# A graph kernel's bf16 parts made inside its projection loop, its sums cleared by GpSimd, and a destination group's extra tiles made in a loop of single turns

## The reference

```python
def gcn_conv(x, W, b, src, dst, norm):          # src, dst with a self loop for each node
    h = x @ W
    return segment_sum(h[src] * norm[:, None], dst, num_segments=N) + b

deg = segment_sum(ones, dst);  dinv = rsqrt(deg);  norm = dinv[src] * dinv[dst]
h = maximum(layernorm(x), 0)
h = relu(gcn_conv(h, W1, b1)); h = relu(gcn_conv(h, W2, b2))
x = x + gcn_conv(h, W3, b3)
h = maximum(layernorm(x), 0)
hv   = h @ W_pre.T + b_pre
filt = edge_attr_50 @ W_rad.T + b_rad
h    = segment_sum(hv[src] * filt, dst, N)
out  = x + silu(h @ W_post.T + b_post)
```

## Time and profile before

| What | us |
| --- | --- |
| median of 3 runs (lowest, highest) | 6050.92 (6018.92, 6109.7) |
| profiled execution, its own time | 6113.65 |
| span of the profiled execution | 6111.8 |
| PE busy (matmuls) | 4563.4 |
| DVE busy | 3084.6 |
| POOL busy | 2929.8 |
| ACT busy | 946.0 |

### The profile page before, as it was taken

How to read it: one execution, slowest core, us unless ns; L and a number is a source line. 1 busy time by engine, 2 the same in 40 slices (tenths; PEclk the granted TensorE clock), 3 DMA queues, 4 the chain that set the end, 5 groups by cost and what they waited for, 6 DMA issues and landing times.

```text
span 6111.8 us, 111789 instructions
## 1 busy us (share of the span) xinstructions
PE 4563.4 (75%) x31388; PEld 3521.4 (58%) x31389; DVE 3084.6 (50%) x8559; ACT 946.0 (15%) x2182; POOL 2929.8 (48%) x3028
## 2 busy tenths in 40 slices
PE   6955777888888885999876999556666666566665
PEld 4742234555555565888665888355555555555554
DVE  6766777777777764444435444542222222222225
ACT  0000123344455541000020000010000000000002
POOL 0002133444510002666715666347777777777772
PEclk9966999999999995999858999566666666666665
DMA  1000011212211111455313554212222222222221
GB/s 33 0 11 18 27 43 50 64 59 70 71 60 68 73 55 49 157 168 169 104 47 104 170 171 150 38 45 48 46 46 46 48 46 46 46 46 48 46 46 33
DMA packets 158668, 407.12 MB, mean 67 GB/s; under 512 B 67564, under 2 KB 80940, under 8 KB 139124
## 3 DMA queue, kind: packets, MB, share of 16 engines
q1 hardware_dynamic: 62068, 305.32, 14.1%
q0 software_dynamic: 96256, 98.76, 8.6%
HBM read 307.53 MB, written 96.33 MB: 66 GB/s over the span
## 4 chain that ended last, share of the span: by engine, by line
PE 41%; POOL 25%; issue 17%; DVE 11%; DVEq 4%; DMA 1%; SPq 0%; POOLq 0%; ACT 0%; ACTq 0%
POOL rows_flat L510 25%; PE ps L1267 13%; PE ps L1366 6%; PE ps L1379 5%; PE ps L1340 5%; PE ps L1239 5%; DVE sumT L974 4%; PE ps L1256 3%; PE ps L1254 2%; PE ps L1247 2%; PE ps L1225 1%; DVE stage_fn L691 1%; DVEq L1048 1%; DVEq L691 1%; DVE hot L1205 1%
## 5 line engine op out<-in xcount | busy, mean ns | idle before, releaser
L510 POOL DMA_INDIRECT rows_flat<-table,row_stage x3008 | 2916.6, 970 | 2060.7 <-issue 1775.6
L1247 PE MATMUL ps<-hot,msg_flat 128*64 128x160 f32 x3136 | 810.8, 446 | 723.2 <-DVE msg_flat L795 723.2
L1366 PE MATMUL ps<-sumT,stage_fn 128*128 128x392 f16 x3976 | 866.3, 338 | 369.3 <-DVE sumT L974 228.0
L1247 PEld LDWEIGHTS ps<-hot,msg_flat 128*64 128x64 f32 x3136 | 650.4, 215 | 839.1 <-issue 707.1
L974 DVE TENSOR_SCALAR sumT<-stage_fn,sub_start,sumT 128x784 f16<-128x784 f16 x1988 | 895.7, 483 | 0.8 <-issue 0.7
L1366 PEld LDWEIGHTS ps<-sumT,stage_fn 128*128 128x128 f16 x3976 | 312.9, 98 | 901.5 <-issue 609.7
L1267 PE MATMUL ps<-wide,ring 128*128 128x192 bf16 x9800 | 828.3, 246 | 0.0
L587 ACT ACTIVATE ring<-ps 128x784 fp8e4<-128x784 f32 x800 | 657.1, 822 | 1047.9 <-PE ps L1366 1033.4
L1267 PEld LDWEIGHTS ps<-wide,ring 128*128 128x128 fp8e4 x9800 | 805.5, 98 | 8.5
L685 DVE TENSOR_SCALAR hot<-iota,dst_rel 128x160 f32<-128x160 f32 (+1 forms) x3008 | 656.2, 294 | 217.0 <-issue 214.5
L795 DVE TENSOR_TENSOR msg_flat<-rows_flat,ps 128x512 f32<-128x512 f32 x196 | 134.6, 687 | 1017.5 <-DMA rows_flat<-table,row_stage 995.9
(11 more groups left out here) (162 smaller groups left out, 2878.6 us busy)
## 6 DMA issues: line engine op xcount, KB each, us to landing
ring<-counts SPq DMA_DIRECT2D x100, 1568.0 KB
counts<-ring SPq DMA_DIRECT2D x50, 1568.0 KB
rows_flat<-table,row_stage POOLq DMA_INDIRECT x3008
ring<-in_radial SPq DMA_DIRECT2D x196, 200.0 KB
table<-node SPq DMA_DIRECT2D x56, 224.0 KB, 1.9
out<-node SPq DMA_DIRECT2D x13, 224.0 KB
ring<-in_dst SPq DMA_DIRECT2D x1, 784.0 KB
ring<-in_src SPq DMA_DIRECT2D x1, 784.0 KB
```

Source lines behind the costliest of these rows:

```text
L510: nc.gpsimd.indirect_dma_start(out=rows[:, j, k * D:(k + 1) * D], out_offset=None, in_=table[:, :], in_offset=bass.IndirectOffsetOnAxis(ap ...
L1247: s = nc.tensor.matmul(to, of, mats[:, k, :], start=(k == 0), stop=(k == BLOCK_TILES - 1))
L1366: m = nc.tensor.matmul(to[:, c, :], sources[:, :, k], joint[k][:, c * (JOINT // 2):(c + 1) * (JOINT // 2)], start=first, stop=True, skip_g ...
```

## The change

Three edits. First, `project(p)` of layers 0, 1 and 2 makes the parts of a group of windows right behind that group's L1011, inside the same loop; the loop of its own behind it is gone. Second, `sumT` is no longer cleared by DVE: POOL does it, after ACT has staged the last sums of the layer before (`fn_staged`) and ahead of its wait for the table, and DVE waits for the new semaphore `sums_cleared` before the pass. Third, the extras of a sub are made by one loop with one turn in each round, on DVE and on PE. All extras of a sub go to the extra buffer `a % 2`, where a is the sub's number modulo 4; before, pairs of turns alternated between the two buffers, and an odd last one went to buffer 0.

```diff
@@ -282,6 +282,7 @@
         root_wanted = sem("root_wanted")
         root_ready = sem("root_ready")
         sums_done = sem("sums_done")
+        sums_cleared = sem("sums_cleared")
         h_ready = sem("h_ready")
         nf_staged = sem("nf_staged")
         flipped = sem("flipped")
@@ -527,6 +528,9 @@
             pool.wait_ge(mode_ready, 1)
             for p in range(PASSES):
                 at = Pass(pool, p)
+                if p:
+                    pool.wait_ge(fn_staged, (COLLECT(p - 1) + 1) * GROUPS)
+                    nc.gpsimd.memset(sumT[:, :], 0.0).then_inc(sums_cleared, 1)
                 pool.wait_ge(table_written, 16 * GROUPS * (p + 1))
                 with pool.If(at.rounds > 0) if p == REDO else nullcontext():
                     with pool.Fori(0, at.rounds) as i:
@@ -1003,6 +1007,26 @@
                 return ps_z[:, h, 0:GROUP * D].rearrange("p (w f) -> p w f", f=D)
 
             def project(p):
+                settle()
+                at = steps[0]
+
+                def parts_of(g2, h, mine):
+
+                    part = [parts[:, groups(g2 * 2 + h), c * D:(c + 1) * D] for c in range(3)]
+
+                    def after(k):
+                        dve.wait_ge(step, g2 * 8 + (at + h * 4 + k))
+
+                    dve.wait_ge(z_used, g2 * 2 + (PROJECT(p) * GROUPS + h + 3))
+                    after(0)
+                    nc.vector.tensor_copy(part[0], mine).then_inc(step, 1)
+                    after(1)
+                    nc.vector.tensor_tensor(tmp[:, :, :], mine, part[0], ALU.subtract).then_inc(step, 1)
+                    after(2)
+                    nc.vector.tensor_copy(part[1], tmp[:, :, :]).then_inc(step, 1)
+                    after(3)
+                    nc.vector.tensor_tensor(part[2], tmp[:, :, :], part[1], ALU.subtract).then_inc(step, 1)
+
                 with dve.Fori(0, GROUPS // 2) as g2:
                     for h in range(2):
                         mine = node[:, groups(g2 * 2 + h), :]
@@ -1010,30 +1034,11 @@
                         if p < GCN_LAYERS:
                             nc.vector.tensor_tensor(mine, z, over_features(dinv[:, groups(g2 * 2 + h)]),
                                                     ALU.mult).then_inc(z_used, 1)
+                            parts_of(g2, h, mine)
                         else:
                             nc.vector.tensor_tensor(mine, z, over_windows(bias[:, B_PRE, :], GROUP),
                                                     ALU.add).then_inc(z_used, 1)
-                if p:
-                    then(nc.vector.memset(sumT[:, :], 0.0))
-                settle()
                 if p < GCN_LAYERS:
-                    at = steps[0]
-                    dve.wait_ge(z_used, (PROJECT(p) + 1) * GROUPS + 2)
-                    with dve.Fori(0, GROUPS) as g:
-                        mine = node[:, groups(g), :]
-                        part = [parts[:, groups(g), c * D:(c + 1) * D] for c in range(3)]
-
-                        def after(k):
-                            dve.wait_ge(step, g * 4 + (at + k))
-
-                        after(0)
-                        nc.vector.tensor_copy(part[0], mine).then_inc(step, 1)
-                        after(1)
-                        nc.vector.tensor_tensor(tmp[:, :, :], mine, part[0], ALU.subtract).then_inc(step, 1)
-                        after(2)
-                        nc.vector.tensor_copy(part[1], tmp[:, :, :]).then_inc(step, 1)
-                        after(3)
-                        nc.vector.tensor_tensor(part[2], tmp[:, :, :], part[1], ALU.subtract).then_inc(step, 1)
                     steps[0] += 4 * GROUPS
                     settle()
                     dve.drain().then_inc(parts_ready, 1)
@@ -1053,12 +1058,8 @@
                         made = joint_hot(joint_main[a][k], sub, t0 + k)
                     made.then_inc(main_ready, 1)
                     with dve.If(n > 0):
-                        with dve.If(n > 1):
-                            with dve.Fori(0, n >> 1) as m2:
-                                for b in range(2):
-                                    extra_hots(b, sub, extra_tile(t0, m2 * 2 + b))
-                        with dve.If((n & 1) > 0):
-                            extra_hots(0, sub, extra_tile(t0, n - 1))
+                        with dve.Fori(0, n) as m:
+                            extra_hots(a % 2, sub, extra_tile(t0, m))
 
             def keep_found(i, h):
 
@@ -1143,6 +1144,7 @@
             for p in range(PASSES):
                 if p:
                     project(p)
+                    dve.wait_ge(sums_cleared, p)
                 if p < GCN_LAYERS:
                     dve.wait_ge(table_written, 16 * GROUPS * (p + 1))
                 edge_pass(p)
@@ -1410,12 +1412,8 @@
 
                     with pe.If(n > 0):
                         main_begins()
-                        with pe.If(n > 1):
-                            with pe.Fori(0, n >> 1):
-                                for b in range(2):
-                                    extra_tiles(to, b)
-                        with pe.If((n & 1) > 0):
-                            extra_tiles(to, 0)
+                        with pe.Fori(0, n):
+                            extra_tiles(to, a % 2)
                         main_ends()
                     with pe.Else():
                         main_begins()
```

## The result

The kernel before takes 6080.47 us (median of 20 runs, 6015.8 to 6137.39), the changed one 6104.13 (median of 20, 6071.31 to 6125.48). The ratio is 1.007 with a 95% interval of 1.0043 to 1.0097: 42 us longer, 26 to 59. The ratio leaves out the runs that lie more than 1.5% above the fastest of their kernel, five of before's 20 and none of the changed kernel's; the medians of all runs lie 24 us apart, their means 27. The forecast was 6101, 50 us above the 6050.92 known then, and no change that 2% could tell.

A forecast was written before the change was run, and what follows sets the result against it. No engine owns the span, so stages were priced at three places. Terms -39.6 - 86.8 + 0 + 191 + 14 - 14 - 15 sum to +50 us on a median of 6050.92, giving 6101 us; range 6000 to 6180.

The forecast's parts named there:

- Part 1, layer 0, -39.6: Layer 0's projection: parts fit in DVE's idle time, so the build starts at 491.2 instead of 530.82, -39.6 us.
- the closing condition: End of the prediction: wrong if turns on one buffer come under 1.5 us apart, or another engine takes the projections' saved time.
- Layers 1 and 2, -43.4 each: Projection to dense pass: parts end sooner, gathers are late next, PE starts 43.4 us earlier per layer, -86.8 in all.
- Part 2, 0 in layer 3, no cost beside DVE: POOL clearing sumT: layer 3 gains 0 (-4 to 0) as gathers set its pace; the memset costs DVE 0.
- Turns, +191: Build loop: 196 later extra turns wait for PE on one buffer, 1.83 or 1.50 us each, +191 us.
- Lost lead, +14: Build loop: DVE cannot run ahead over subs with two or more extras, +14 us (0 to +30).
- First extras' waits, -14: Build loop: a sub's first extra uses another buffer than its neighbour's, so waits less for PE, -14 us (-27 to 0).
- Code, -15: Build loop: shorter code, 749 rows for 1197, removes the later stop but not the jump's stop, -15 us (-34 to 0).
- low clock: Rival, build loop: PE stays at 1.2 GHz through three rounds, all 196 turns cost 1.83 us; +144, 6195 us; chance 0.10.
- Turns covered: Rival, build loop: 2.4 GHz throughout, no lead lost, first waits and later stops gone; -38, 6013 us; chance 0.19.
- The jump's stop goes: Rival, build loop: 749 rows fit, so 25 stops of 4.8 to 8.7 us go; +50 - 69, 6032 us; chance 0.08.
- GpSimd's memset stops DVE: Rival, clearing of sumT: POOL's memset stops DVE or comes late; +32, 6133 us; chance 0.05.

The follow-up runs named there:

- e2: Kernel before with only the parts moved inside the projection's loop, DVE still clearing sumT behind it; 5992.56 us, ratio 0.9892.
- e8: Kernel before, unchanged, run once more for another profile; 6018.41 us in one run.
- e3: Changed kernel with the pair loop of before for the extra tiles, so only parts and clearing moved; 5960.4 us, ratio 0.9853.
- e6: Changed kernel plus a never-entered pair loop in each sub of DVE's code, restoring the loop's 1197 rows; 6154.04 us, ratio 1.0178.
- e4: As e3, but a sub's pair loop and odd tile begin on buffer a%2 instead of buffer 0; 5947.0 us, ratio 0.9823.
- e1: Kernel before with only the single-turn loops for extra tiles on DVE and PE; 6194.14 us, ratio 1.0237.
- e9: As e3, with the third part of each node value left out and its array cleared once; 5964.39 us, ratio 0.9819.

## Why the prediction was right

It was right in size, and luck had a share in it twice. The 6101 is +50 on a median of three runs, 6050.92, that lay 30 us below the median of 20; the same +50 on 6080.47 would be 6130. And the change itself, +50 for a measured +24 to +42, is a sum whose two large parts missed in opposite directions: Parts 1 and 2 gain less than forecast, Part 3 costs less.

- *Bound by stages, three places.* Held.
- *Part 1, layer 0, -39.6.* Measured -39.5 where both projections run at 1.2 GHz (e2), -20.6 where the one without parts would have run at 2.4 (e8's 79.2 us against 58.6 from first product to first main tile). The step that failed is "PE is not held up, and the cover is DVE's idle 4.11 us". It is true of layers 0 to 2 in the profile of before, which had drawn 1.2 GHz; at 2.4 GHz a group is 2.6 us on PE and 3.6 on DVE (the forecast had 3.8), DVE is the bound, and then the clock goes too. So the closing condition, that another engine picks up the time that the projections give back, was met in part, by PE.
- *Layers 1 and 2, -43.4 each.* The mechanism held to 2 us (45.6 at 1.2 GHz, gathers late next), its size again only at that clock; from 147.6 to some 120 it is 27.
- Weighing both cases by the 7 of 12 draws at 2.4 GHz, -39.6 and -86.8 become about -28 and -70: **-98 instead of -126**. e3 measured -89 (64 to 113), by the means -105.
- *Part 2, 0 in layer 3, no cost beside DVE.* Held.
- *Turns, +191.* The sum of turns rose by 204. The turn itself was priced 0.09 us too long at either clock (1.74 and 1.41, not 1.83 and 1.50). By its own words the prediction is wrong if turns on one buffer come closer than 1.5 us, and at 2.4 GHz they do: "a turn costs what a pair did" is not exact. The sum is above +191 all the same, because the clock was up only from the second half of the second round on, not from sub 16.
- *Lost lead, +14.* Measured 0: e6 against e4, 203.8 us in the loop for 203.1 in the turns (subs 0 to 127).
- *First extras' waits, -14.* e4 has -17 in its loop.
- *Code, -15.* The term that was mis-sized: e6 puts it at **50 us**. The stop at the jump stayed, as forecast, and the later one went. But that one had been misread: it is not in some ten rounds and five subs on, but in three, two subs on, 9.3 us in all. What the term left out is that the stops at the jump became shorter too, by 26.5 us over all 24.
- Together for Part 3, 204 - 17 - 50 - 13 (the last unexplained) is the **+124** of the loops, **instead of +176** (e1: +143 by its ratio, +125 by the means). With -98 that is +26; e1 and e3 together are +54 by the ratios and +19 by the means, where the change itself measured +42 and +27.

Of the rivals, the *low clock* had met its own condition, no rise before sub 16, and yet its 6195 was not reached: its turns were 1.74 us, and the code gave back 50. *Turns covered* was wrong outright, in subs 0 to 15 above all. *The jump's stop goes* did happen in part: each stop became shorter, 26.5 us in all of its 69, and none went. *GpSimd's memset stops DVE* did not.

What stays open: some 13 us of the gain in subs 128 to 511 that neither DVE's code length (e6) nor the buffers (e4) explain. PE's loop is shorter in the change as well, and that was not tried alone. Open too are 11 of e6's 50 us, and what makes a projection start at 1.2 or at 2.4 GHz.

## What to carry to other kernels

Before work is put under another engine's idle time, price that idle time at both clock levels: DVE's cover of 4.1 us a group was 1.9 us in 7 of 12 projections, and filling it cost the clock as well. One profile is one draw for each projection, and here its fourth one already showed the other level; when a kernel's own runs lie in steps, look for the stage that drew differently before trusting any term read from it. Two buffers in turn are worth keeping (203 us here), also where the loop that uses them is longer, and starting each sub on the other buffer costs nothing. Shorter code pays only where the engine that runs it sets the pace: behind sub 512 its length made no difference.

## What the runs showed of the hardware

- The granted clock in one and the same projection of one and the same kernel is 1.2 GHz in one execution and 2.4 in the next: 4.8 or 2.6 us a group, 28 to 30 us a projection, four projections a run.
- PE held 2.4 GHz through a projection of 33 us that it ran without a gap (e8, e9), and dropped to 1.2 where DVE held it to 3.6 us a group, in 14 of 14 projections within 4 us of a first gap of 0.5 to 0.7 us. The reverse doesn't hold: without a gap it also stayed at 1.2 for a whole projection (before, layers 0 to 2).
- 448 dead rows in a DVE loop of 749 and the condition before them cost 50 us in 25 rounds (e6): 12 instead of 8 instruction packets a round, stops of 4.8 instead of 3.8 us at the eighth to the fifteenth jump, and in four rounds a second one of about 2.9.
- GpSimd subtracts 128x448 in 1.03 us; beside it DVE's subtraction of the same size took 1.2 to 1.4 us instead of 0.62, beside GpSimd's memset it kept 0.62.
